# Keys of five head pairs made in an earlier stage, and weighted sums a step later, in an eight-stage Trainium2 kernel

## The reference

```python
def _L3_xattn_ref(x, context, Wq, Wkv, null_kv, Wout, ln_scale, ln_bias):
    HEADS, DH = (16, 64)
    q = _split_heads(einsum('bnd,df->bnf', x, Wq))          # x is normalised
    k, v = split(einsum('bmc,cf->bmf', context, Wkv), 2)     # from the context alone
    k = concatenate((null key, k)); v = concatenate((null value, v))
    attn = softmax(einsum('bhid,bhjd->bhij', q * DH ** -0.5, k))
    out = einsum('bhij,bhjd->bhid', attn, v)
    out = einsum('bnf,fd->bnd', merge_heads(out), Wout)
    return layernorm(out) * ln_scale + ln_bias
```

## Time and profile before

| | |
|---|---|
| median of 3 runs | 1111.31 us (1111.29 to 1115.84) |
| profiled execution: its time | 1108.31 us |
| profiled execution: its span | 1106.6 us |
| null-key stage, from the scores of step 1 to the last weighted sums | 868.54 to 1027.51 us in the span |
| TensorE busy, share of the span | 88% (976.5 us) |
| a load of 256 KB (32 of them), median from issue to landing | 3.4 us |
| unmasked attention, from the end of the stage before | 290 to about 433 us |

### The profile page before, as it was taken

One profiled execution on the slowest core, in us unless ns is written; L12 is line 12 of the kernel. 1 busy time (PEld: TensorE's weight loads), 2 busy tenths in 40 slices (PEclk: granted clock), 3 DMA queues, 4 the chain that ended last, 5 costly groups with the idle time before them and its releaser, 6 DMA issues.

```text
span 1106.6 us, 18238 instructions
## 1 busy us (share of the span) xinstructions
PE 976.5 (88%) x5958; PEld 720.9 (65%) x5958; DVE 818.1 (74%) x1980; ACT 636.6 (58%) x1594; POOL 431.7 (39%) x664
## 2 busy tenths in 40 slices
PE   5689999999669998878999999996899999998587
PEld 4447887888413345756777777775677877777465
DVE  7857888888677872699989998768665667674663
ACT  3275766776317775367787877873144566664121
POOL 9241222221121110236676766767050465654200
PEclk9698999999859998899999999997799999999789
DMA  5531111121152210300000000303001000003000
GB/s 213 144 121 41 40 39 39 51 62 57 44 161 83 83 40 20 153 1 1 1 1 1 1 1 1 152 1 122 1 1 55 24 1 2 1 20 134 1 1 19
DMA packets 32254, 53.55 MB, mean 48 GB/s; under 512 B 4192, under 2 KB 24448, under 8 KB 31008
## 3 DMA queue, kind: packets, MB, share of 16 engines
q1 hardware_dynamic: 29616, 50.03, 13.5%
q10 hardware_dynamic: 2544, 2.36, 0.7%
HBM read 45.33 MB, written 6.88 MB: 47 GB/s over the span
## 4 chain that ended last, share of the span: by engine, by line
PE 64%; DVE 16%; ACT 9%; issue 6%; DMA 2%; POOL 1%; SPq 1%; DVEq 0%; ACTq 0%
PE psum L1783 9%; PE psum L1410 7%; PE psum L1400 7%; ACT region_d L1845 4%; PE psum L2574 3%; PE psum L2503 3%; PE psum L1813 3%; PE psum L400 2%; PE psum L444 2%; DVE region_d L1981 2%; ACT region_c L1862 2%; PE psum L1769 2%; PE psum L2477 2%; PE psum L2519 2%; DVE null_work L2676 2%
## 5 line engine op out<-in xcount | busy, mean ns | idle before, releaser
L1783 PE MATMUL psum<-gated_parts 128*128 128x512 f32 x768 | 193.6, 405 | 17.2 <-DVE region_d L1981 13.3
L1783 PEld LDWEIGHTS psum<-gated_parts 128*128 128x128 f32 x768 | 139.4, 191 | 67.6 <-DVE region_d L1981 34.4
L2074 POOL TENSOR_TENSOR region_d<-region_d 128x256 f32<-128x256 f32 x126 | 94.5, 750 | 92.8 <-DVE region_d L1981 90.7
L1475 ACT ACTIVATE rounds_work<-psum,region_c 128x512 f32<-128x512 f32 x128 | 85.2, 688 | 30.4 <-PE psum L1400 26.7
L834 DVE TENSOR_REDUCE work<-psum 128x1 f32<-128x512 f32 x128 | 81.8, 685 | 21.7 <-PE psum L400 20.3
L1400 PE MATMUL psum<-parts,split 128*128 128x512 f32 x384 | 94.7, 396 | 0.5 <-DVE parts L1523 0.5
L1597 POOL CAST parts<-rounds_work 128x1024 fp32r<-128x1024 f32 x32 | 37.1, 1159 | 145.1 <-ACT rounds_work L1475 145.1
L1410 PE MATMUL psum<-parts,split 128*128 128x512 f32 x384 | 93.3, 392 | 0.0
L1845 ACT ACTIVATE region_d<-psum,gated_work 128x128 f32<-128x128 f32 x256 | 76.0, 451 | 27.0 <-issue 22.3
L1529 DVE TENSOR_TENSOR parts<-rounds_work,parts 128x1024 fp32r<-128x1024 f32 x64 | 76.3, 1221 | 20.6 <-POOL parts L1597 19.4
L1845 ACT ACTIVATE region_d<-psum,ctx 128x128 f32<-128x128 f32 x256 | 73.0, 375 | 25.6 <-PE psum L1783 16.1
(11 more groups left out here) (457 smaller groups left out, 2183.5 us busy)
## 6 DMA issues: line engine op xcount, KB each, us to landing
rounds_work<-cw_rows SPq DMA_DIRECT2D x32, 256.0 KB, 3.4
region_a<-in_l1v SPq DMA_DIRECT2D x8, 512.0 KB, 4.0
region_b_last<-in_l1o SPq DMA_DIRECT2D x1, 4096.0 KB, 12.1
region_a<-in_l2f SPq DMA_DIRECT2D x1, 4096.0 KB, 13.3
region_b_last<-in_l3f_small SPq DMA_DIRECT2D x1, 4096.0 KB, 12.9
region_a<-in_l3f SPq DMA_DIRECT2D x1, 2080.0 KB, 7.3
region_c<-in_l0f SPq DMA_DIRECT2D x1, 2076.0 KB, 12.2
region_c<-in_l3x SPq DMA_DIRECT2D x1, 2048.0 KB, 8.7
```

Source lines behind the costliest of these rows:

```text
L1475: act.activation(H[g % 2][:, f, :], bank[f], ACT.Gelu_apprx_tanh, bias=W("b1")[:, (g % E) * FT + f:(g % E) * FT + f + 1]).then_inc(h_ready ...
L1783: ins = pe.matmul(bank[2 * (n % 2) + c], src[a][:, t * P:(t + 1) * P], weights[b][:, piece(c)], start=m == 0, stop=m == len(PASSES) - 1)
L2074: pool.tensor_tensor(tile[:, 0:2, :], tile[:, 0:2, :], tile[:, 2:4, :], ALU.add).then_inc(k.pool_chain, 1)
```

## The change

Keys of pairs 3 to 7 (both halves, ten pieces of 128 x 512) are made in the unmasked attention stage and stored in DRAM. Their matmuls are plain fp32 there: 40 of them (`quarter`), each of 256 columns over one half of the context's features, four to a piece. Eight stand at the start of that stage, twenty between the projections and the first pass, and one in each of the first 12 steps. ScalarE copies the ten pieces out. SyncE stores them in the loop and, in the null-key stage, loads each before it is needed, into the words where the parts of the key weights had been. There ScalarE and VectorE make the high and low parts from the loaded piece in SBUF, as before from PSUM.

In the null-key stage, further: the weighted sums of step n are done in step n + 1, into bank 7; so the projections have bank 6 alone. A step's first projection stands between the scores and those sums, a second one behind the turns. For pairs 3 to 7 the plan is q half 0, then v, then q half 1, then v. VectorE does both maxima first, and then reciprocal, copy, reciprocal, copy. ScalarE does both exponentials first, as before, then one projection, the sums of the step before, and the rest. The output products of the last pair stand in steps 0, 1 and 3 of it, none in step 2 and twice as many in step 3.

```diff
+class NullKeysAhead:
+    PAIRS = range(3, 8)
+    BANKS = (4, 5, 4, 7, 5, 6, 4, 5, 6, 4)
+    IN_FRONT, AHEAD = 8, 28
+    HALVES = 10
+    QUARTERS = 40
...
+    def quarter(self, pe, j):
+        k = self.k
+        n, q, c = j // 4, j % 4 // 2, j % 2
+        pair, h = self.PAIRS[n // 2], n % 2
+        if j == 0:
+            pe.wait_ge(*self.loaded.at(16))
+        if j % 4 == 0 and self.BANKS[n] in self.BANKS[:n]:
+            last = max(m for m in range(n) if self.BANKS[m] == self.BANKS[n])
+            pe.wait_ge(*self.copied.at(last + 1))
+        first = h * HALF + q * HALF // 2
+        ins = pe.matmul(k.bank[self.BANKS[n]][:, q * HALF // 2:(q + 1) * HALF // 2], self.weights[:, c, pair * P:(pair + 1) * P],
+                        k.ctxT[:, c, first:first + HALF // 2], start=c == 0, stop=c == 1)
...
+    def store(self, sp, n):
+        sp.wait_ge(*self.copied.at(n + 1))
+        sp.dma_start(self.k.dram["null_keys"][n * P:(n + 1) * P, :], self.keys[n]).then_inc(self.stored.semaphore, 16)
...
 def packed_attention(...):     # tensor
+        if not masked:
+            for j in range(keys.IN_FRONT):
+                keys.quarter(pe, j)
         k.norm.tensor(pe, use, k.xn)
...
         else:
+            for j in range(keys.IN_FRONT, keys.AHEAD):
+                keys.quarter(pe, j)
             pe.wait_ge(*rest.at(first_of(3)))
...
+                if not masked and s == 0:
+                    pe.wait_ge(*keys.copied.at(keys.HALVES))
                 second_pass(*divmod(s, STEPS))
...
+            if not masked and i < keys.QUARTERS - keys.AHEAD:
+                keys.quarter(pe, keys.AHEAD + i)
...
 def packed_attention(...):     # scalar
+            if not masked and pair == 1:
+                for n in range(2, 5):
+                    keys.copy(act, n)
...
+            if not masked and i % 4 == 3 and i < keys.QUARTERS - keys.AHEAD:
+                keys.copy(act, (keys.AHEAD + i) // 4)
...
 def packed_attention(...):     # sync, unit v
                 k.load_piece(sp, "l1v", v, UNITS * B)
+                for n in range(2 * v - 2, 2 * v):
+                    if 0 <= n < keys.HALVES:
+                        keys.store(sp, n)
...
 def null_key_attention(...):
+        if p + 1 in keys.PAIRS:
+            plan = ((("q", 0), ("k", 0)), (("v", 0), ("k", 1)), (("q", 1),), (("v", 1),))
...
     def bank_of(n):
-        return k.bank[1 + n] if n < 2 else k.bank[6 + n % 2]
+        return k.bank[1 + n] if n < 2 else k.bank[6 + n % 2] if n < FIRST else k.bank[6]
...
             if n >= 4:
-                pe.wait_ge(proj_sb, n - 1)
-                if n >= 6 and MADE[n - 2][0] != "v":
-                    pe.wait_ge(*proj_low.at(LOWS[n - 2]))
+                at = HERE.index(n)
+                same = HERE[at - 1 if at > FIRST else at - 2]
+                pe.wait_ge(proj_sb, same + 1)
+                if n >= 6 and MADE[same][0] != "v":
+                    pe.wait_ge(*proj_low.at(LOWS[same]))
...
+        for n in range(STEPS):
+            p, b = divmod(n, B)
+            if n + 1 < STEPS:
+                scores(*divmod(n + 1, B))
+            here = [m for m in MADE_IN[p][b] if m in HERE]
+            for m in here[:1]:
+                project(m)
+            if n > 0:
+                weighted_sums(n - 1)
+            for i in range(2):
+                turn(2 * n + i)
+            for m in here[1:]:
+                project(m)
+            if p + 1 == PAIRS and b != 2:
+                h = b // 2
+                pe.wait_ge(*cleared.at(h + 1))
+                pe.wait_ge(av_sb, B * (PAIRS - 2) + b + 1)
+                for t in range(TPB * b, TPB * (b + 1)) if h == 0 else range(4, 8):
+                    output(t, range(PAIRS - 1))
+        turn_null_weights(0)
+        weighted_sums(STEPS - 1)
...
             if more:
                 maxima(g + 2)
+                maxima(g + 3)
+                reciprocals(g + 2)
             copy_turned(g)
             if more:
-                maxima(g + 3)
-                reciprocals(g + 2)
+                reciprocals(g + 3)
             copy_turned(g + 1)
-            if more:
-                reciprocals(g + 3)
-            p, b = divmod(g // 2, B)
-            if b < 2:
-                for n in MADE_IN[p][b]:
+            for n in here:
+                if MADE[n][0] != "v":
                     low_projections(n)
```

196 lines of the change are left out of this document (128 added, 68 removed).

## The result

The changed kernel takes 1128.94 us (median of 4, 1123.70 to 1134.69) against 1113.57 us of the kernel before in the same comparison: 15.4 us more. The ratio estimated from the executions is 1.016 (95% interval 1.012 to 1.020; the quotient of the two medians is 1.014), so it is slower, clear of the noise but by less than 2%. Its profiled execution took 1123.70 us, 15.4 above that of the kernel before (1108.31), so the profile holds the whole loss: 14.4 of it in the span (1121.0 against 1106.6), 1.0 outside.

What follows compares the result with a forecast made beforehand. It took TensorE to bound steps with q and k, and a circle through maxima and copies the steps without projection. Null-key stage +4.6 and front -3.4 gave +1.2 us: 1109.5, 1112.5 as a median, range 1100 to 1120.

Steps and rivals of the forecast that it cites:

- pairs 1 and 2: Null-key stage, keys still made there: k waits in bank 6 for q's subtraction; +4.4 us a pair, first step -0.3.
- pairs 3 to 6: Null-key stage, keys loaded: 18.4 us a pair, v waiting for q's subtraction; -0.95 us each, -3.8 for four.
- pair 7: Null-key stage, no v beside it: paced by VectorE and the exponentials, -2.5 us.
- last pair: End of the null-key stage: output products moved out of its third step, sums of its last step wait 1.8; +2.4 us.
- front: Unmasked stage: quarters fill TensorE's idle time, so the clock there rises to 2.4 GHz; -3.4 us.
- null-key stage: Sum of its pairs: 8.8 - 0.3 - 3.8 - 2.5 + 2.4 = +4.6 us.
- the second rival: Unmasked front: the clock does not rise, first pass 7 us late, 12 steps need 1.7; 1126.5 us, chance 0.14.
- The third rival: Null-key steps: every extra change of array shape drains TensorE, 0.38 us in 10 to 20 steps; 1116 to 1120, chance 0.16.
- The first rival: Null-key stage: VectorE subtracts before TensorE needs the bank, pairs 1 and 2 keep 19.36; 1095.6 us, chance 0.22.
- Loads: Null-key stage: key loads cost nothing, most asked for 18 us ahead of use; uncovered, each would cost 3.4 us.

Runs made afterwards that it cites:

- quarters_before_pass: Changed kernel with the twelve quarters of the first pass's loop moved ahead of that pass; 1135.33 us, 1.027 of the kernel before.
- order_only: Kernel before with the whole new null-key order and one bank, no keys made ahead, stored or loaded; 1148.98 us, ratio 1.035.
- two_banks_16_together: Changed kernel with keys of pairs 6 and 7 only, two projection banks, last pair's outputs and both projections ahead of the turns; 1110.80 us, 0.999 of before.
- two_banks_keys: Changed kernel with projections in banks 6 and 7 in turn, sums in bank 5 ahead of the first projection; 1117.63 us, 1.005 of before.
- front_only: Kernel before with the new front; keys made and stored but unused, null-key stage as before; 1119.97 us, ratio 1.011.
- keys_only: Kernel before with the new front and loaded keys, keeping its null-key plan, order and two banks; 1119.10 us, ratio 1.011.

## Why the prediction was wrong

The forecast was 1112.5 us with 1100 to 1120 around it, and no measurable change as the likeliest case (0.49); it is 1128.9 and slower, for which I had 0.27. Term by term, in the profiled execution:

| term | forecast | measured |
|---|---|---|
| pairs 1 and 2 | +8.5 | 25.48 + 25.58 - 38.72 = +12.3 |
| pairs 3 to 6 | -3.8 | 76.97 - 77.44 = -0.5 |
| pair 7 | -2.5 | 18.26 - 19.36 = -1.1 |
| last pair | +2.4 | 25.41 - 23.44 = +2.0 |
| front | -3.4 | 0.3 + 5.2 = +5.5 |

The five terms were forecast at +1.2 together and measured +18.2. Two steps failed, each by about as much: the front (-3.4 for +5.5) and the null-key stage (+4.6 for +12.7). Either alone would have put the time just outside the range, at 1120.6 or 1121.4 counted as in the forecast's sum. The 4.5 us that came back behind the start of the second pass, which the table leaves out, I take for scatter (535.0 to 542.0 in 18 profiles); they are luck and no merit of the forecast.

**The first failed step is the clock of the front.** "With the gaps filled I expect 2.4 GHz there" held for 290 to 309 us (1.00 in the row, and the first k product took 0.87 from start to start instead of 1.65, as said) and failed where it mattered: the first pass ran at half clock as in the earlier trace rows. I had taken the level in the pass for a result of the idleness ahead of it. In the changed kernel that may still hold in part: TensorE rested 2.29 us for the loads just before the pass, and the clock was 0.66 in the first us behind it and 0.50 in the next. But `quarters_before_pass` shows that the pass does not need that rest to lose the clock. There TensorE worked up to the pass with a single rest of 0.20 us, the pass began at full clock, and by 320 us it had fallen all the same.

```profile
314.00:318.00 4.00, 2.58 (x10) 0.75 (x8) 2.93 (x5) 0.60 (x1) 0.00 (x0) 1.00 0.70 197
318.00:322.00 4.00, 3.18 (x6) 0.59 (x6) 3.80 (x7) 0.00 (x0) 0.00 (x0) 0.68 0.73 201
322.00:326.00 4.00, 3.35 (x7) 0.69 (x7) 3.63 (x7) 0.02 (x1) 0.00 (x0) 0.50 0.19 52
```

What TensorE did before that fall was the pass itself: two matmuls and then a wait of 0.2 to 0.8 us for VectorE, again and again. The quarters ahead of the pass did not keep its clock up. Then the second rival's sum applies in part: 2 x 0.43 + 0.83 = 1.7 a step, where 1.84 was measured as a mean, since a quarter between two groups of another shape took 1.15; its 3.6 us for the twelve was 5.2. Its other half, 7 us for quarters at half clock ahead of the pass, did not come, since there the clock was full. The flaw was that the rival tied the two to one clock: the stretch ahead and the pass have a level each.

**The second failed step is the sum of the null-key stage,** 8.1 us short. Pairs 1 and 2 were right in kind (k waits for q's subtraction, 1.69 us; forecast 1.9) and short in size: at full clock the four steps are 7.14, 7.80, 5.21 and 4.57 in `order_only`, and I had 6.95, 7.5, 4.9 and 4.4. That is 1.0 a pair, and the low clock behind a wait is another 0.8 in pair 2 (25.58, where `quarters_before_pass` has 24.75 at full clock), which I did not think of.

**Pairs 3 to 6** were forecast at 18.4 and took 19.25. Three sizes were off. q takes 0.90 when sums follow (941.44 to 942.34) and not 0.78, which I had read from a q that k follows; turns take 1.03 ahead of scores (943.35 to 944.38) and not 0.84. And the subtraction of the loaded key takes up to 1.31, not 0.79. With two banks and the sums first the turns ahead of the scores still take 0.97 and the subtraction up to 0.97, but the pairs are 18.4 long, so I take it that it is at the one bank that these sizes turned into waits. The third rival, that each extra change of shape costs 0.38, was thus right in kind and too dear: 0.12 and 0.19 in a step. The Trainium skill, "TensorEngine Tiling (Array Packing)", section Key Properties, says that a change of tiling mode drains the engine. The traces agree in that a group takes longer from start to start when one of another shape follows: k takes 1.39 us when turns follow (`two_banks_16_together`), 1.48 when sums follow (before) and 1.56 when scores follow (`two_banks_keys`).

**Pair 7** was forecast 2.5 us shorter than before and is 1.1 shorter. Of the difference 0.8 is the low clock behind ScalarE's wait: in `quarters_before_pass` the same code has 1.00 throughout pair 7 and takes 17.5 us (998.01 to 1015.52). **The last pair** was near: +2.0 for +2.4, and the wait for VectorE's copy 1.51 for 1.8.

**The first rival, that the one bank does not hold,** is refuted by the wait of 1.69 us ahead of k, and `two_banks_keys` gets 13.6 us back with a second bank.

**Loads and loss outside the span.** No load of a key was waited for, as forecast. What the stores cost behind the second pass can't be told from the scatter of that stretch. The 1.0 us outside the span was not forecast. On record it goes with the loaded keys: the time outside the span is 1.7 to 2.2 us in all executions of kernels that load none in the null-key stage, and 1.8 to 3.8, mostly above 2.0, in those that do. Why is open.

Not settled: by the tables the front of 40 quarters costs 5.5 to 6.8 us of a profile, while the medians of `front_only` and `keys_only` stand 9 to 10 us above before. With starts that scatter by 12 us and four or five executions, the rest may be chance; I have no run that tells. Nor was the traffic of the ten stores tried apart from the quarters.

## What to carry to other kernels

Before a buffer is taken from a producer to free it for something else, follow one round trip of that buffer through every queue that must release it (here ScalarE behind two exponentials, then VectorE behind two copies): the wait of 1.7 us in each step with q and k was more than the 1.49 of k that a loaded key saves a step. Ask of work put into idle time not only whether the engine is idle but at which clock it will run in that very stretch; up to 24 quarters were free at full clock ahead of the pass, and those inside it cost 0.43 us each. And when an engine's list gets shorter, look for the circle that comes next: under the old order the saved k became a wait for a copy, and only with two banks and the sums a step later was a pair worth 1.3 us.

## What the runs showed of the hardware

- **VectorE and GpSimd exclude each other on SBUF.** The subtraction of two SBUF operands on VectorE takes 0.71 us when GpSimd's multiplication has 0.16 us to go, 0.97 with 0.42 to go (`two_banks_keys`), 1.31 with 0.75 and 1.52 with 0.97: each time it ends 0.55 us behind GpSimd. VectorE's subtraction of q, which has a source in PSUM, takes 0.68 with 0.76 to 0.99 us of such a multiplication to go. The Trainium skill, "SBUF — State Buffer", section Who interferes with whom, says that a VectorE instruction with two SBUF inputs contends with a GpSimd instruction that reads SBUF, and that the ports they share are an exclusive lock; the trace agrees.
- **The low clock can outlast a busy TensorE.** From 314 to 336 us of the changed kernel the records show it busy for 22.00 of 22 us at 0.50. The clock rose within a us or two of the start of the second pass (335.19). In the kernel before it stayed at 0.50 for 6 us into the second pass, from 329.06 to 335.
- **Some waits are followed by a low stretch and others are not.** In the null-key stage of the changed kernel the clock fell to 0.50 behind waits of 2.42, 1.70 and 1.68 us (pairs 1, 2 and 7), and stayed at 1.00 behind those of 1.69 us at 884.36 and 901.31. In `order_only` it fell once, behind the 2.41 of pair 1, and behind none of the later waits of 1.70; `quarters_before_pass` kept 1.00 behind the 1.69 of its pair 7. What tells them apart is open.
- **The first stages scatter.** The transposes of the unmasked stage stood between 293.3 and 305.4 us in 18 profiles, though the code ahead of them differs by no more than the load of the weights and the eight quarters, with a granted clock of 0.73 to 0.95 between 50 and 100 us.
